# First turns of an attention pipeline: zeroing, first root and one weight split moved, unread products put into TensorE's gaps

## The chip, the cores and the metric

The kernel runs on one core of one Trainium2 chip. The metric is the device time of one launch in microseconds; the median of three runs is compared. The profile shows one further execution, taken by the hardware profiler.

## The reference

One transformer layer over 64 sequences of 128 tokens with a width of 512, in f32.

```python
h = base_weight[x] + lora_A.T[x] @ lora_B.T            # gather, rank 16
n = layernorm(h)                                       # no gain
cq, ckv = layernorm(n @ W_dq), layernorm(n @ W_dkv)   # 128 wide, with gain and bias
q, (k, v) = cq @ W_uq, ckv @ W_ukv                     # 16 heads of 32
h = h + softmax(causal(q k^T / sqrt(32))) v @ W_o.T
h = h + experts(layernorm(h))                          # shared expert and 8 of 16 routed experts
```

## The kernel before

The work falls into an attention phase (to about 943 us) and an expert phase. Both go over 16 groups of 4 sequences; a group is 512 tokens, four tiles of 128 rows. This document is about the first turns of the attention phase.

**Turns.** The attention phase is a software pipeline written out by hand: turn `n` runs from -2 to 16. A turn has 16 steps. In turn `n` the softmax of group `n` is done (16 slots, one a step: four heads of one tile), the `c` vectors of group `n + 1` are finished and its `q`, `k`, `v` begun, and the front of group `n + 2` is made: embedding `h`, its normalisation, the transposes `xt`, and the down projection `wd`. So turn -2 has only a front, for group 0; turn -1 has the front of group 1 and the first `ct`, `k` 0 and `q` 0 of group 0; turn 0 is the first one with softmax, and the output projection `out` begins in turn 1.

**Order of the work.** Each engine has its own instruction list with semaphores between them and works in order. Two banks of PSUM (`work`) pass the products of all parts of the front: `MIDWAY` and `END` say in which step a part comes, `place` gives the bank and how often it must have been drained, `empty` waits for that, and `was_read` frees it. TensorE's order of parts in turn -1 is `art` 0 and 1, `h` 0 to 3, `ct` 0 and 1, `k` 0, `xt` 0 to 2, `wd` 0, `xt` 3, `wd` 1, `q` 0. In turn 0 the `h` parts stand in steps 2, 3 and 5 between scores and transposes of probabilities.

**f32 products.** A product of f32 operands is made of three products of split operands (`split_matmul`, L487 to L489): each operand is stored as a rounded high part and the rest (`_hi`, `_lo`). The weights are split once at the start, in three pieces (`W_PIECES`): ScalarE rounds (L753) and VectorE subtracts (`split_weights`, L763). Pieces 0 and 1 arrive in the tile `k_diag`, piece 2 (the output projection's weights) in `res`.

**k_diag.** The keys are stored in a block-diagonal tile that must be zero where no key stands. GpSimd zeroes it once (L470), in step 8 of turn -2, behind the first gather for the next group; the first copies of `k` wait for it in turn -1.

**Root.** The inverse standard deviation is a seed from the exponent (`rsqrt_seed`, L66 to L71, four operations on VectorE) and three Newton steps of four dependent operations each (`rsqrt_steps`, L78 to L84), run by GpSimd in step 7 for `h` and in step 3 for `c`. The normalisation of `h` (L808, four operations, one a tile) waits for the whole of it.

**Gathers.** GpSimd issues four indirect DMAs a group (L439); the low-rank columns of the gathered rows are copied and split in `split_ar` (L769 to L772).

**Softmax in turn 0.** VectorE takes the row maxima for two slots at once (`row_max`, L877), ScalarE the exponentials (L698), VectorE the reciprocals (L883), GpSimd the scaling (L454), TensorE the transposes (L591), ScalarE the copies (L705), TensorE the products with `v` (L603).

Of the kernel before, what the change touches and what calls it, by code (L numbers as in the profile page):

```python
# [86 lines left out]
def shift_of(pool, done, count, mean, y, t, shift, passed):  # L87
# [28 lines left out]
END = {0: (("k", 1), ("q", 2)), 2: (("h", 0), ("h", 1)), 3: (("h", 2),), 4: (("v", 2),), 5: (("h", 3),)}  # L116
FRONT = ("art", "h", "xt", "wd")

STATS_AT, NORM_AT, C_NORM_AT, SPLIT_AT = (3, 6), 10, 5, 14
# [18 lines left out]
def is_turn(n, which):  # L138

    return isinstance(n, int) and n == which  # L140
# [78 lines left out]
def attention(nc, shared, w_ffn, w_gate, biases, table, tok, lora_b, w_attn, ln, h2):  # L219
# [3 lines left out]
    with ExitStack() as ctx:  # L223
# [127 lines left out]
        def was_read(instruction, n, part, i, drains=DRAINS):  # L351
            instruction.then_inc(work_free[place(n, part, i)[0]], drains)

        def slots_of(n):

            return range(0 if any(is_turn(n, k) for k in (-2, -1, GROUPS)) else SLOTS)
# [64 lines left out]
        @block.gpsimd  # L421
        def _(pool):
            pool.memset(ident[:, :], 0.0).then_inc(consts, 1)
            pool.memset(mask[:, :, :], 0.0).then_inc(consts, 1)
            pool.wait_ge(consts, 2)
            pool.affine_select(out=ident[:, :], in_=ident[:, :], compare_op=ALU.not_equal, fill=1.0,
                               base=0, pattern=[[-1, P]], channel_multiplier=1).then_inc(ident_done, 1)

            pool.affine_select(out=mask[:, :, :], in_=mask[:, :, :], compare_op=ALU.is_ge, fill=MASKED,
                               base=0, pattern=[[0, HPC], [-1, P]],  # L430
                               channel_multiplier=1).then_inc(ident_done, 1)
            pool.wait_ge(tok_step, 4)

            def pick(g):
                pool.tensor_copy(tok_now[:, :], tok_fix[:, bass.ds(g * TILES, TILES)]).then_inc(tok_picked, 1)
                wait_alone(pool, tok_picked, g + 1, pool_passed)

            def gather(g, t):
                pool.indirect_dma_start(  # L439
                    out=gath[:, t, :], out_offset=None, in_=table,  # L440
                    in_offset=bass.IndirectOffsetOnAxis(ap=tok_now[:, t:t + 1], axis=0),
                ).then_inc(gathered[t], 16)

            def wait_gathered(g):
                for t in range(TILES):
                    pool.wait_ge(gathered[t], 16 * (g + 1))

            def newton_of(base, n):
                rsqrt_steps(pool, newton, base, nw[:, 1, 0:n], nw[:, 3, 0:n], nw[:, 4, 0:n],
                            pool_passed)  # L450

            def normalise_probs(n, s):
                pool.wait_ge(inv_done, SLOTS * n + s + 1)
                pool.tensor_tensor(probs[:, s % RING, :, :], probs[:, s % RING, :, :],  # L454
                                   inv[:, s % RING, :].rearrange("p (h o) -> p h o", o=1).to_broadcast([P, HPC, P]),
                                   ALU.mult).then_inc(probs_done, 1)

            def turn(n, side):
                for step in range(SLOTS):
                    if has_slot(n, step - NORM_LAG):  # L460
                        normalise_probs(n, step - NORM_LAG)
                    if GATHER_AT <= step < GATHER_AT + TILES and has_part(n, "h", 0) and not is_turn(n, GROUPS - 3):
                        if step == GATHER_AT:
                            wait_gathered(n + 2)
                            drained(pool, n, "h", TILES - 1)
                            pick(n + 3)
                        gather(n + 3, step - GATHER_AT)
                        if is_turn(n, -2) and step == GATHER_AT:
                            pool.wait_ge(w_lo_done, len(W_PIECES))
                            pool.memset(k_diag[:, :, :, :, :], 0.0).then_inc(k_zeroed, 1)  # L470
                    if step == RSTD_AT and has_part(n, "xt", 0):
                        newton_of(2 * NEWTON_OPS * (n + 2), TILES)
                    if step == C_RSTD_AT and has_part(n, "ct", 0):
                        newton_of(2 * NEWTON_OPS * (n + 1) + NEWTON_OPS, 2 * TILES)

            pick(0)
            for t in range(TILES):
                gather(0, t)
            for n in range(-2, GROUPS + 1):
                turn(n, n % 2)  # L480

        @block.tensor
        def _(pe):
# [58 lines left out]
            def up(n, part, i):  # L542

                if is_turn(n, -1):
                    pe.wait_ge(w_lo_done, 2)
                elif is_turn(n, 0) and part == "v":
                    pe.wait_ge(w_lo_done, len(W_PIECES))
                if i == 0 and part != "v":
                    pe.wait_ge(cT_lo_done, 2 * (n + 1) + (1 if part == "q" else 2))
                if part == "v":  # L550
                    a, b = pair(cT_hi, cT_lo, 1, i * P, (i + 1) * P), wts(W_UV, D)
                else:
                    a = wts((W_UQ if part == "q" else W_UK) + i * P, P)
                    b = pair(cT_hi, cT_lo, int(part == "k"), 0, TOK)
                return split_matmul(bank_of(n, part, i), a, b, True, True)

            def out_proj(n, side, t, chunks=range(DC)):
                if not is_turn(n, GROUPS):
                    pe.wait_ge(oT_lo_done, DC * n)
                for m in chunks:  # L560
                    if is_turn(n, GROUPS):
                        pe.wait_ge(oT_lo_done, DC * (n - 1) + m + 1)
                    mm = split_matmul(bank_of(n, "out", t),
                                      pair(oT_hi[:, 1 - side], oT_lo[:, 1 - side], m, t * P, (t + 1) * P),
                                      wts(W_O + m * D, D), m == 0, m == DC - 1)
                return mm
# [27 lines left out]
            def heads_out(n, s):  # L594
# [10 lines left out]
                                   start=True, stop=True)  # L605
                mm.then_inc(o_full, 1)

            def work_on(n, side, uses):
                for part, i in uses:
                    if has_part(n, part, i):  # L610
                        empty(pe, n, part, i)
                        if part == "art":
                            mm = ar_turn(n, i)
                        elif part == "h":
                            mm = embed(n, i)
                        elif part == "xt":
                            mm = x_turn(n, i)
                        elif part == "wd":
                            mm = down(n, i)
                        elif part == "ct":  # L620
                            mm = c_turn(n, i)
                        elif part == "out" and is_turn(n, GROUPS) and i < 2:
                            mm = out_proj(n, side, i, range(2, DC))
                        elif part == "out":
                            mm = out_proj(n, side, i)
                        else:
                            mm = up(n, part, i)
                        mm.then_inc(work_full[place(n, part, i)[0]], 1)
# [130 lines left out]
        def _(dve):  # L759
# [33 lines left out]
            def seed_of(base, var, n):  # L793
                rsqrt_seed(dve, newton, base, var, nw[:, 0, 0:n], nw[:, 1, 0:n],
                           nw[:, 2, 0:n].bitcast(I32), nw[:, 4, 0:n])

            def h_seed(g):
                dve.wait_ge(h_moments, TILES * (g + 1))
                seed_of(2 * NEWTON_OPS * g, moments[:, :, 1], TILES)

            def c_seed(g):
                dve.wait_ge(c_moments, 2 * TILES * (g + 1))
# [122 lines left out]
            def turn(n, side):  # L925
                front, rows = has_part(n, "xt", 0), has_part(n, "ct", 0)
                for step in range(SLOTS):
# [24 lines left out]
                    if front:  # L952
                        if step == SPLIT_AT and is_turn(n, GROUPS - 2):
                            prepare_gate()
                        elif step == SPLIT_AT and not is_turn(n, GROUPS - 3):
                            split_ar(n + 3)
                        if step == STATS_AT[0]:
                            h_stat(n, 0)
                            h_stat(n, 1)
                        if step == STATS_AT[1]:  # L960
                            h_stat(n, 2)
                            h_stat(n, 3)
                            h_moment(n + 2)
                            h_seed(n + 2)
                            if is_turn(n, -2):
                                split_weights(2)
                        if step == NORM_AT:
                            normalise(n + 2)

            dve.memset(ar[:, :, :].bitcast(F32), 0.0).then_inc(ar_zeroed, 1)  # L970
            dve.wait_ge(tok_loaded, 16)
# [802 lines left out]
```

## Time and profile before

| | us |
|---|---|
| median of three runs | 2520.44 (2519.99 to 2520.92) |
| the profiled execution | 2518.29 |
| its span, first to last instruction | 2516.5 |
| TensorE busy | 2421.6 (96%) |
| ScalarE busy | 1814.8 (72%) |
| VectorE busy | 1707.6 (68%) |
| GpSimd busy | 1134.3 (45%) |
| mean granted TensorE clock | 0.995 |

PE is TensorE, PEld its weight loads, DVE VectorE, ACT ScalarE, POOL GpSimd and SP SyncE. Busy time is summed over instructions that the profiler recorded; matmuls are pipelined, so a product's duration includes its way through the array, and the distance between two starts says more. A time in the views below is counted from the span's start.

### The profile page before, as it was taken

Reading aid. Unit: us, or ns where it says so; the run is one execution under the profiler, and the core shown is the slowest. Engines: PE = TensorE matmul, PEld = TensorE weight load, DVE = VectorE, ACT = ScalarE, POOL = GpSimd, SP = SyncE. Lnnn points to the kernel's source line nnn. Section 1 sums busy time; section 2 is a strip of 40 time slices with the busy share of each in tenths; the row PEclk is TensorE's granted clock in tenths of the full one; section 3 lists DMA queues with packets and bytes.
Section 4 is the critical chain, followed back from the end, with each engine's and each line's share of the span. In section 5 each row is a group of like instructions: output and inputs, shape, how many; then the busy total and the mean of one; then the engine's idle time right before and its main releaser. Section 6 shows DMA issues by size and latency. Waiting matters only on the chain.

```text
span 2516.5 us, 47561 instructions
## 1 busy us (share of the span) xinstructions
PE 2421.6 (96%) x13632; PEld 1866.1 (74%) x13632; DVE 1707.6 (68%) x3604; ACT 1814.8 (72%) x4593; POOL 1134.3 (45%) x1285
## 2 busy tenths in 40 slices
PE   3899999999999999999999999999999999999999
PEld 2666666666666766678878878878878888888887
DVE  6777777777777764857657657657657657657655
ACT  1777777777777786868668668668668768767766
POOL 4444444444444332336436435445435445445445
PEclk8999999999999999999999999999999999999999
DMA  3222222222222122522222322221221321321321
GB/s 108 69 68 69 69 81 69 73 69 73 73 81 77 60 65 80 164 85 76 92 72 70 96 80 58 96 87 51 97 88 50 101 85 49 101 88 46 101 74 60
DMA packets 99830, 198.24 MB, mean 79 GB/s; under 512 B 10928, under 2 KB 10928, under 8 KB 99568
## 3 DMA queue, kind: packets, MB, share of 16 engines
q1 hardware_dynamic: 94576, 179.29, 21.6%
q0 software_dynamic: 5120, 17.31, 2.8%
q8 instruction: 67, 1.10, 0.2%
q14 instruction: 67, 0.55, 0.1%
HBM read 145.66 MB, written 50.86 MB: 78 GB/s over the span
## 4 chain that ended last, share of the span: by engine, by line
issue 30%; POOL 26%; PE 2%; DVE 1%; ACT 1%; POOLq 1%; DVEq 0%; ACTq 0%
POOL t_lo L1280 24%; POOL sh_lo L1280 2%; POOLq L1278 1%; DVE ps_u L1647 0%; DVE f_lo L1672 0%; DVE t L1654 0%; ACT t_hi L1499 0%; PE fwork L1295 0%; PE ps_g L1295 0%; ACT square L1482 0%; PE ps_g L1297 0%; PE ps_g L1296 0%; PE ps_u L1297 0%; PE ps_u L1295 0%; PE ps_u L1296 0%
## 5 line engine op out<-in xcount | busy, mean ns | idle before, releaser
L1280 POOL TENSOR_TENSOR t_lo<-t,t_hi 128x512 fp32r<-128x512 f32 x512 | 662.9, 1295 | 413.9 <-ACT t_hi L1499 413.8
L454 POOL TENSOR_TENSOR probs<-probs,inv 128x512 f32<-128x512 f32 x256 | 266.4, 1042 | 473.9 <-DVE inv L883 472.7
L1647 DVE TENSOR_TENSOR ps_u<-ps_u,square 128x512 f32<-128x512 f32 x512 | 357.0, 697 | 155.9 <-ACT square L1486 139.6
L1499 ACT ACTIVATE t_hi<-t 128x512 fp32r<-128x512 f32 x512 | 320.6, 626 | 112.0 <-PE ps_y L1297 66.8
L1654 DVE TENSOR_TENSOR t<-ps_u,res 128x512 f32<-128x512 f32 x512 | 354.0, 691 | 55.5 <-DVE ps_u L1647 22.4
L1482 ACT ACTIVATE square<-ps_g 128x512 f32<-128x512 f32 x544 | 319.6, 587 | 91.9 <-PE ps_g L1297 90.2
L698 ACT ACTIVATE probs<-ps_s,nmax 128x128 f32<-128x128 f32 x1024 | 364.0, 382 | 20.8 <-DVE nmax L877 19.7
L1486 ACT ACTIVATE square<-square 128x512 f32<-128x512 f32 x544 | 344.2, 633 | 17.3
L698 ACT ACTIVATION_READ_ACCUMULATOR probs<-ps_s,nmax 128x1 f32 x1024 | 228.0, 223 | 0.0
L1295 PE MATMUL ps_y<-t_hi,f_hi 128*128 128x512 f32 x512 | 208.4, 407 | 14.1 <-POOL t_lo L1280 12.6
L1280 POOL TENSOR_TENSOR sh_lo<-t,sh_hi 128x512 fp32r<-128x512 f32 x32 | 41.9, 1310 | 389.7 <-ACT sh_hi L1499 389.7
L1297 PE MATMUL ps_u<-xl_hi,f_lo 128*128 128x512 f32 x512 | 200.1, 391 | 0.0
L1296 PE MATMUL ps_y<-t_lo,f_hi 128*128 128x512 f32 x512 | 200.1, 391 | 0.0
L1295 PE MATMUL ps_u<-xl_hi,f_hi 128*128 128x512 f32 x512 | 199.9, 390 | 0.2 <-DVE t L1654 0.2
L1297 PE MATMUL ps_y<-t_hi,f_lo 128*128 128x512 f32 x512 | 199.9, 390 | 0.0
L1295 PE MATMUL ps_g<-xl_hi,f_hi 128*128 128x512 f32 x512 | 199.8, 390 | 0.0
L1297 PE MATMUL ps_g<-xl_hi,f_lo 128*128 128x512 f32 x512 | 199.5, 390 | 0.0
L1296 PE MATMUL ps_g<-xl_lo,f_hi 128*128 128x512 f32 x512 | 199.2, 389 | 0.0
L1296 PE MATMUL ps_u<-xl_lo,f_hi 128*128 128x512 f32 x512 | 199.2, 389 | 0.0
L705 ACT ACTIVATE pT<-ps_t 128x512 f32<-128x512 f32 x256 | 158.4, 619 | 27.3 <-PE ps_t L591 25.2
L877 DVE TENSOR_REDUCE nmax<-ps_s 128x8 f32<-128x1024 f32 x128 | 155.9, 1218 | 27.4 <-PE ps_s L582 26.9
L591 PE MATMUL ps_t<-ident,probs 128*128 128x128 f32 x1024 | 163.9, 283 | 8.1 <-ACT pT L705 4.9
(196 smaller groups left out, 5367.7 us busy)
## 6 DMA issues: line engine op xcount, KB each, us to landing
res<-w_rows SPq DMA_DIRECT2D x256, 256.0 KB, 3.2
h<-rows SPq DMA_DIRECT2D x64, 256.0 KB, 2.0
res<-h SPq DMA_DIRECT2D x64, 256.0 KB, 2.8
h<-res SPq DMA_DIRECT2D x64, 256.0 KB, 2.0
rows<-h SPq DMA_DIRECT2D x16, 1024.0 KB, 5.6
keep<-h SPq DMA_DIRECT2D x16, 1024.0 KB, 7.2
out<-keep SPq DMA_DIRECT2D x64, 256.0 KB, 2.3
keep<-in_w_ffn SPq DMA_DIRECT2D x12, 512.0 KB, 3.6
```

What stands on the lines that cost most here:

```text
L454: pool.tensor_tensor(probs[:, s % RING, :, :], probs[:, s % RING, :, :], inv[:, s % RING, :].rearrange("p (h o) -> p h o", o=1).to_broadca ...
L591: mm = pe.transpose(ps_t[:, j * P:(j + 1) * P], probs[:, s % RING, j, :], ident[:, :])
L698: e = act.activation(probs[:, s % RING, j, :], ps_s[:, b, x, i, y, :], ACT.Exp, bias=nmax[:, b, x, i, y:y + 1], accum_out=total[:, s % RIN ...
L1280: pool.tensor_tensor(lo, t[:, t_slot(j), :], hi.bitcast(F32), ALU.subtract).then_inc(t_lo_done, 1)
L1295: pe.matmul(o, a_hi, b_hi, start=first, stop=False)
L1296: pe.matmul(o, a_hi, b_lo, start=False, stop=False)
L1297: return pe.matmul(o, a_lo, b_hi, start=False, stop=last)
L1482: act.activation(square[:, j % 2, :], ps_g[:, j % 2, :], ACT.Relu).then_inc(relu_done, 1)
L1486: act.activation(square[:, j % 2, :], square[:, j % 2, :], ACT.Square).then_inc(square_done, 1)
L1499: act.activation(dst, t[:, t_slot(j), :], ACT.Copy).then_inc(t_hi_done, 1)
L1647: dve.tensor_tensor(dst, product, square[:, j % 2, :], ALU.mult).then_inc(t1_done, 1)
L1654: dve.tensor_tensor(t[:, t_slot(j), :], ps_u[:, u_bank(j), :], w_all[:, e % 2, :], ALU.mult).then_inc(t_done, 1)
```

## The change

- The zeroing of `k_diag` moves from step 8 of turn -2 to the start of GpSimd's list, behind the four gathers of group 0. It waits for two weight splits there instead of three.
- The Newton steps of the first `h` root (turn -2) are done by VectorE, right behind its seed, instead of by GpSimd. All later roots stay on GpSimd.
- VectorE's split of weight piece 2 moves from step 6 of turn -2 to step 1 of turn 0. The wait of TensorE for this piece moves from the `v` products of turn 0 to the first output projection in turn 1.
- `keep_awake` puts products on TensorE whose result nothing reads: in turn -1 ten before `ct` 0, eight before `k` 0 and four before `xt` 0, into the bank `ps_t`; in turn 0 two before each of the four `h` parts, into `ps_o`. Each multiplies the bf16 identity with the 128x512 bf16 mask.

```diff
+AWAKE = {("ct", 0): 10, ("k", 0): 8, ("xt", 0): 4}
...
+        def before_softmax(n):
+
+            return is_turn(n, -2)
...
                         gather(n + 3, step - GATHER_AT)
-                        if is_turn(n, -2) and step == GATHER_AT:
-                            pool.wait_ge(w_lo_done, len(W_PIECES))
-                            pool.memset(k_diag[:, :, :, :, :], 0.0).then_inc(k_zeroed, 1)
-                    if step == RSTD_AT and has_part(n, "xt", 0):
+                    if step == RSTD_AT and has_part(n, "xt", 0) and not before_softmax(n):
                         newton_of(2 * NEWTON_OPS * (n + 2), TILES)
...
                 gather(0, t)
+            pool.wait_ge(w_lo_done, 2)
+            pool.memset(k_diag[:, :, :, :, :], 0.0).then_inc(k_zeroed, 1)
...
                     pe.wait_ge(w_lo_done, 2)
-                elif is_turn(n, 0) and part == "v":
-                    pe.wait_ge(w_lo_done, len(W_PIECES))
...
             def out_proj(n, side, t, chunks=range(DC)):
+                if is_turn(n, 1) and t == 0:
+                    pe.wait_ge(w_lo_done, len(W_PIECES))
...
+            def keep_awake(bank, count):
+
+                for k in range(count):
+                    pe.matmul(bank, ident_b[:, :], mask[:, :, :], start=True, stop=True)
+
             def work_on(n, side, uses):
                 for part, i in uses:
                     if has_part(n, part, i):
+                        if is_turn(n, -1) and (part, i) in AWAKE:
+                            keep_awake(ps_t[:, :], AWAKE[part, i])
+                        if is_turn(n, 0) and part == "h":
+                            keep_awake(ps_o[:, :], 2)
                         empty(pe, n, part, i)
...
+            def newton_of(base, n):
+                rsqrt_steps(dve, newton, base, nw[:, 1, 0:n], nw[:, 3, 0:n], nw[:, 4, 0:n], dve_passed)
+
             def h_seed(g):
                 dve.wait_ge(h_moments, TILES * (g + 1))
                 seed_of(2 * NEWTON_OPS * g, moments[:, :, 1], TILES)
+                if before_softmax(g - 2):
+                    newton_of(2 * NEWTON_OPS * g, TILES)
...
                             h_seed(n + 2)
-                            if is_turn(n, -2):
-                                split_weights(2)
                         if step == NORM_AT:
                             normalise(n + 2)
+                        if is_turn(n, 0) and step == 1:
+                            split_weights(2)
```

## Rows read from the trace of the kernel before

**Rows 1.** Windows: engine busy us (instructions), then granted clock, DMA share, GB/s.
```profile
30.00:50.00 20.00, 12.27 (x71) 10.64 (x71) 13.09 (x34) 3.85 (x7) 8.30 (x10) 0.99 0.22 54
50.00:70.00 20.00, 10.69 (x40) 8.29 (x40) 14.05 (x35) 5.11 (x8) 9.93 (x25) 0.50 0.32 95
...
77.29:128.31 51.02, 44.34 (x350) 30.07 (x350) 40.46 (x100) 41.94 (x160) 24.90 (x44) 1.00 0.21 64
128.31:182.00 53.69, 52.55 (x397) 36.65 (x397) 40.75 (x91) 42.67 (x163) 23.93 (x43) 1.00 0.25 80
```

**Rows 2.** Timeline of GpSimd, turn -2: start us, us, engine, line, operation, tiles.
```profile
10.26 2.51 POOL L439 DMA_INDIRECT gath<-in_table,tok_now  x1 [0.30 <-issue]
24.18 2.17 POOL L78 TENSOR_TENSOR nw<-nw 128x4 f32<-128x4 f32 x1 [11.42 <-DVE nw L71]
...
29.65 0.20 POOL L84 TENSOR_TENSOR nw<-nw 128x4 f32<-128x4 f32 x1
...
31.89 3.52 POOL L470 MEMSET k_diag<- 128x4096 f32 x1
```

**Rows 3.** Timeline of VectorE, turn -2; the last row from a narrower window.
```profile
15.74 0.20 DVE L769 CAST ar<-gath 128x64 fp32r<-128x64 f32 x1 [3.79 <-DMA gath<-in_table,tok_now]
...
23.93 0.17 DVE L71 TENSOR_SCALAR nw<-nw 128x4 int32<-128x4 int32 x1
24.01 2.28 DVE L763 TENSOR_TENSOR w_lo<-res,w_hi 128x2048 fp32r<-128x2048 f32 x1
29.89 5.81 DVE L808 TENSOR_SCALAR keep<-rows,moments,nw 128x512 f32<-128x512 f32 x4 [3.60 <-POOL nw L84]
...
31.27 4.43 DVE L808 TENSOR_SCALAR keep<-rows,moments,nw 128x512 f32<-128x512 f32 x1
```

**Rows 4.** Timeline of TensorE, turn -2.
```profile
36.35 1.12 PE L518 MATMUL work<-ident,keep 128*128 128x128 f32 x4 [3.82 <-DVE xT_lo L813]
```

**Rows 5.** Timeline of TensorE, turn -1.
```profile
54.82 1.94 PE L538 MATMUL work<-ident,c 128*128 128x128 f32 x8 [3.81 <-DVE c L831]
60.31 0.77 PE L487 MATMUL work<-cT_hi,w_hi 128*128 128x512 f32 x1 [3.55 <-DVE cT_lo L845]
...
65.83 1.11 PE L518 MATMUL work<-ident,keep 128*128 128x128 f32 x4 [0.63 <-DVE xT_lo L813]
...
70.23 0.28 PE L488 MATMUL work<-w_lo,xT_hi 128*128 128x256 f32 x1
...
71.18 0.60 PE L518 MATMUL work<-ident,keep 128*128 128x128 f32 x4
```

**Rows 6.** Timeline of VectorE in the expert phase, around two Newton steps.
```profile
1056.77 1.13 DVE L82 TENSOR_SCALAR fnw<-fnw 128x4 f32<-128x4 f32 x1
...
1059.35 0.15 DVE L78 TENSOR_TENSOR fnw<-fnw 128x4 f32<-128x4 f32 x1
...
1060.05 0.16 DVE L84 TENSOR_TENSOR fnw<-fnw 128x4 f32<-128x4 f32 x1
```

**Rows 7.** Timeline of VectorE, turn -1.
```profile
57.31 1.52 DVE L840 TENSOR_SCALAR cT<-work,gains 128x512 f32<-128x512 f32 x2
...
62.58 1.90 DVE L808 TENSOR_SCALAR keep<-rows,moments,nw 128x512 f32<-128x512 f32 x4
```

**Rows 8.** Timeline of GpSimd, turn -1.
```profile
61.59 0.20 POOL L84 TENSOR_TENSOR nw<-nw 128x4 f32<-128x4 f32 x1
...
62.78 2.17 POOL L439 DMA_INDIRECT gath<-in_table,tok_now  x1 [0.83 <-POOL tok_now L435]
```

**Rows 9.** Timelines of turn 0: TensorE twice, VectorE, ScalarE.
```profile
77.29 0.60 PE L577 MATMUL ps_s<-mask,ident_b 128*128 128x512 bf16 x2
...
86.72 0.60 PE L577 MATMUL ps_s<-mask,ident_b 128*128 128x512 bf16 x2
...
83.02 1.19 DVE L877 TENSOR_REDUCE nmax<-ps_s 128x8 f32<-128x1024 f32 x1
...
84.34 0.39 ACT L698 ACTIVATE probs<-ps_s,nmax 128x128 f32<-128x128 f32 x1
```

## The prediction

> **What bounds the kernel now.** I first cut the span into stretches by turn [rows 1]. In turn 1 (128.31 to 182 us) TensorE is busy 52.55 of 53.69 us, while before the softmax starts no engine is near full: TensorE does 12.27 us of the 20 from 30 to 50 and 10.69 of the 20 behind them, and VectorE, the busiest, has gaps too. Until turn 0 the kernel is a chain of single steps, and what this chain gains or loses moves all of the rest. Next I read each engine in order of time. In turn -2 the chain is gather, split of the low-rank columns, `h`, statistics, root, normalise, transpose, split, `wd`. The root is twelve dependent operations on GpSimd: its first took 2.17 us beside VectorE's third weight split, and the last ends at 29.85 [rows 2, 3]. Then VectorE normalises; the fourth tile begins at 31.27 and lasts 4.43 us, until just after GpSimd's zeroing of `k_diag` (31.89 to 35.41) has ended [rows 2, 3]. VectorE works in order, so the split of `xT` stands behind it, and TensorE's third transpose, which waits for that split, comes only at 36.35 [rows 4]. In turn -1 the granted clock is 0.50 (1.2 GHz) over the whole stretch from 50 to 70, after a stretch in which TensorE was idle two fifths of the time; it is 1.00 (2.4 GHz) in turns 0 and 1 [rows 1]. The `wd` products of turn -1 show the price: the first sixteen begin 0.21 us apart, the last eight, from 70.23 to 71.18, 0.119 [rows 5].
>
> **First root on VectorE, and the weight split out of the way.** Removed: GpSimd's 5.7 us (24.18 to 29.85). Added: the same twelve operations on VectorE. The expert phase runs a step of four there from 1059.35 to 1060.05, plus 0.16, so about 0.89 us a step [rows 6] and 2.7 for three. The seed's last operation starts at 23.93 [rows 3], so the root ends near 26.8 instead of 29.85: 3.1 us. The four gathers for turn -1 now go out beside it. One scalar operation of such a root took 1.13 us instead of 0.17 beside GpSimd's work [rows 6]; three of them held like that would cost 2.9. But the four normalises at 62.58, beside a gather issued at 62.78, took 1.90 us, and it was the gather that was stretched to 2.17 [rows 7, 8]. That is the nearer row, and I take nothing.
>
> **Zeroing at the start.** It waits for the second weight split and is queued behind the last gather's issue (10.26 + 2.51 = 12.77), so it runs from 12.8 to 16.3 [rows 2]. It no longer stands beside the normalise: from the start of normalise to the third transpose turn -1 needs 65.83 - 62.58 = 3.25 us [rows 5, 7], turn -2 needed 36.35 - 29.89 = 6.46 [rows 3, 4]. That gains 3.2 us. But the small casts of the gathered rows start at 15.74 [rows 3], inside the zeroing's new place. If it holds them as it held the fourth normalise, they start at 16.35, a loss of 0.6; if not, 0. The held normalise is the nearest row, so I take 0.6.
>
> The Trainium skill, SBUF — State Buffer, section "SBUF: two separate sides", speaks against both moves: GpSimd and VectorE lock one shared port pair for a whole instruction, whoever comes first, and VectorE needs it in a two-port mode. By this rule the casts are held, and so can be the root's three scalar operations behind the gathers; that is rival (e) below.
>
> Turn -2 comes to 3.1 + 3.2 - 0.6 = 5.7 us. Where in `wd` the clock rises is open; a slow product costs 0.094 more than a fast one, and with some eleven of 24 slow before, all fast would gain 1.0 and five more slow lose 0.5. I take 5.6 for turn -2, bounds 4.0 and 7.0.
>
> **Unread products in turn -1.** Ten before `ct` 0, eight before `k` 0, four before `xt` 0, each 128x512 in bf16. Two of that shape, the mask products, take 0.53 us at 2.4 GHz, the time to the next product [rows 9]; at the low level a product of 512 columns costs twice the 0.21 of one of 256. So ten cost 2.7 to 4.3 us, and TensorE is idle 3.81 before `ct` 0; eight cost 2.1 to 3.4 in a gap of 3.55; four cost 1.1 to 1.7 in one of 1.3 [rows 5]. Fast, all lie inside the gaps; slow, the first overruns by 0.5 and the last by 0.4. The ten and the `ct` products (1.94) make one dense stretch of 6 us, longer than the 4.4 between the third transpose at 65.83 and the first fast product at 70.23 [rows 5], so I expect the high level from `k` 0 on. What that buys: at `ct` nothing, since VectorE reaches the gains only at 57.31 [rows 7], after `ct` has ended at 56.76 [rows 5]. `k` 0 ends 0.7 earlier, and more would not help: the normalise at 62.58 next waits for GpSimd's second root, which ends at 61.79 [rows 7, 8]. From there to the end of `wd` 0 it was 71.18 - 62.58 = 8.6 us. The first transposes save 0.45 of it, the third one 0.4, and 24 fast products take 2.9 us instead of 4.5: 2.5 together. So 3.2 us for turn -1; bounds -0.5 (the clock stays low, the overrun is paid) and 4.0.
>
> **What turn 0 pays.** The third weight split (2.28 us) [rows 3] now stands on VectorE in front of the second row maximum at 83.02 [rows 9]. Behind that maximum stand the second reciprocal and two additions to `h`, and ScalarE's third exponentials wait for it. They go from 84.34 to 86.5. An `h` product needs the bank that the first addition frees, so it comes 1.4 us later, and the scores behind it start at 88.1 instead of 86.72 [rows 9]. GpSimd's first scaling and the transposes that wait for it lie inside the same delay. ScalarE is busy 41.94 of the turn's 51.02 us, VectorE 40.46 [rows 1], and in the first part of the turn in particular they hand work to one another without a pause, so I let nothing be made up. GpSimd's `c` root sits behind its third scaling and comes 2.0 late. The unread products, two before each `h`, cost 0.53 a pair: three pairs fall into waits, the last is added. For split and products together I take 2.0 us; below, 0.5 if the idle time on TensorE (51.02 - 44.34 = 6.7 us over the turn) takes it up; above, 2.3 + 4 x 0.53 = 4.4.
>
> The waits that the change adds for the third split cost nothing: the first load of `res` queues on SyncE behind the stores of `h` of the same turn, which are later than the split's new end near 85.3, and the output projection comes in turn 1. What used to cover the split was the wait for GpSimd's root; that cover is gone, and its whole price is in turn 0's term.
>
> **Sum.** -5.6 - 3.2 + 2.0 = -6.8 us. The profiled execution took 2518.29 us, 1.8 more than its span of 2516.5, so its successor would take 2511.5. The median of the runs is 2520.44, 2.15 above the profiled one; the forecast for the median is 2520.44 - 6.8 = 2513.6.
>
> **The rivals.** (a) The clock stays low in turn -1. For it: the unread products alone must lift it, and before them it had just fallen; against it: the dense stretch of 6 us. Then -5.6 + 0.5 + 2.0 = -3.1, 2517.3. (b) Turn 0's delay is paid at its upper bound, since VectorE, ScalarE and GpSimd hand the probabilities round in a fixed order; against it, the idle time on TensorE. Then -5.6 - 3.2 + 4.4 = -4.4, 2516.0. (c) The split's delay returns: if the fixed order throws 2.28 us in at four of the eight row maxima of turn 0, it costs 9.1, and the time is 2520.44 - 8.8 + 9.1 = 2520.7. Slower begins at 8.8 us lost in turn 0, slower by over 0.2% at 13.8; that TensorE is idle 6.7 us there and only one instruction is added speaks against it. (d) Everything falls well: the zeroing holds nothing, the clock is high early in both turns, turn 0 takes up the split: -7.0 - 4.0 + 0.5 = -10.5, 2509.9. (e) GpSimd's gathers hold the first root's scalar operations for 2.9 us, as the 1.13 us row would have it: -3.9, 2516.5; the normalise beside a gather speaks against it. That the change does nothing at all at the first root is all but excluded: VectorE's wait of 3.60 us before the normalise ends with GpSimd's last root operation [rows 3].
>
> **How the numbers follow.** The forecast has 0.55, (a) 0.15, (b) 0.12, (c) 0.03, (d) 0.10, (e) 0.05. A difference of 0.2%, 5.0 us, is about what a measurement of this kernel can tell from no change, so the border is at 2515.4. The forecast's own range is 2511.6 to 2515.6, nearly all of it faster, and (d) is faster too; (a), (b) and (e) lie within 0.2% with some of their spread beyond it. That gives faster 0.68, same 0.29, slower 0.03. The range of eight in ten goes up to half a microsecond beyond (a) and down to 2510.8, which leaves out (c) and most of (d): 2510.8 to 2517.8.
>
> **What would show it.** The casts at 16.35; normalise of turn -2 at about 27.4 and its four operations in 1.9 us; the third transpose near 30.7; the granted clock at 1.00 from `k` 0 of turn -1 on; the scores of turn 0 at about 68.5 instead of 77.29; turn 0 some 53 us long, and turn 1 as it was. The forecast is wrong if the root on VectorE takes over 4 us, if the low clock comes back behind the unread products, or if turn 0 grows by over 4 us or not at all.

## The result and the profile after

The median went from 2519.89 us (20 runs, 2517.65 to 2521.46) to 2516.1 us (20 runs, 2513.25 to 2519.15): 3.8 us less, ratio 0.9986, 95% interval 0.9980 to 0.9993. That is a small gain, clear of zero but within 0.2%. The forecast was 2513.6, range 2510.8 to 2517.8. The profiled execution took 2515.29 us with a span of 2513.5.

The runs of the change differ in TensorE's clock, and the time goes with it: the three with a mean granted clock of 0.999 took 2513.3 to 2514.6 us, the two with 0.998 took 2513.3 and 2516.9, the thirteen with 0.997, the profiled one among them, 2515.3 to 2518.0, and the two with 0.996 took 2518.5 and 2519.2. Times near the forecast came only at 0.998 and 0.999.

The main reading is the lead of the changed kernel at landmarks, its start time against that of before. Turn -2 first; this is the timeline of VectorE in the changed kernel, its line numbers shifted a little against before:

```profile
15.46 0.20 DVE L782 CAST ar<-gath 128x64 fp32r<-128x64 f32 x1 [3.47 <-DMA gath<-in_table,tok_now]
...
23.83 0.17 DVE L71 TENSOR_SCALAR nw<-nw 128x4 int32<-128x4 int32 x1
24.03 0.16 DVE L78 TENSOR_TENSOR nw<-nw 128x4 f32<-128x4 f32 x1
...
26.57 0.16 DVE L84 TENSOR_TENSOR nw<-nw 128x4 f32<-128x4 f32 x1
26.77 1.95 DVE L826 TENSOR_SCALAR keep<-rows,moments,nw 128x512 f32<-128x512 f32 x4
```

The root takes 2.7 us (24.03 to 26.73) and nothing holds it, though a gather was issued at 24.12 and one at 25.37: the two scalar operations beside them take 0.17 us each. In the seed before it one scalar operation did take 0.34 instead of 0.17 us and ended with the issue of the gather of 22.85. The normalise starts 3.12 us earlier and takes 1.95 instead of 5.81 us [rows 3]. The timeline of GpSimd has the zeroing, which ends at 15.57, as the casts begin:

```profile
12.06 3.51 POOL L482 MEMSET k_diag<- 128x4096 f32 x1 [0.90 <-DVE w_lo L776]
```

TensorE's third transpose, at 30.04, is 6.31 us ahead of [rows 4]. Turn -1 on TensorE:

```profile
44.83 3.16 PE L615 MATMUL ps_t<-mask,ident_b 128*128 128x512 bf16 x9 [0.33 <-issue]
48.33 1.16 PE L542 MATMUL work<-ident,c 128*128 128x128 f32 x8 [0.35 <-DVE c L849]
49.33 1.89 PE L615 MATMUL ps_t<-mask,ident_b 128*128 128x512 bf16 x8
53.82 0.77 PE L491 MATMUL work<-cT_hi,w_hi 128*128 128x512 f32 x1 [2.60 <-DVE cT_lo L863]
...
55.24 1.93 PE L615 MATMUL ps_t<-mask,ident_b 128*128 128x512 bf16 x4
56.97 1.15 PE L522 MATMUL work<-ident,keep 128*128 128x128 f32 x8
59.17 0.66 PE L522 MATMUL work<-ident,keep 128*128 128x128 f32 x4 [1.05 <-DVE xT_lo L831]
...
62.74 0.60 PE L522 MATMUL work<-ident,keep 128*128 128x128 f32 x4
```

The ten products (nine are recorded) run from 44.8, and the clock is up from 46.9, but the eight end at 51.2, TensorE idles 2.60 us, and at 53.8 the clock falls again, so `k` 0 runs at the low level: it gains nothing over [rows 5]. Behind it the clock is up from 57.2, and the whole of `wd` 0 is fast: from the normalise at 56.09 to the transpose at 62.74 it takes 6.65 us instead of 8.6. The scores of turn 0 begin at 69.14, 8.15 us ahead of [rows 9] (8.4 in truth: the first of the two mask products is not recorded here, at both ends of the turn, so the turn's length is right). The windows, columns as in [rows 1], the last one being turn 0 from its first scores to those of turn 1:

```profile
30.00:50.00 20.00, 16.19 (x85) 11.66 (x87) 12.59 (x45) 3.47 (x7) 2.54 (x12) 0.91 0.12 46
50.00:70.00 20.00, 15.36 (x91) 10.97 (x92) 11.88 (x41) 6.88 (x12) 8.25 (x17) 0.91 0.27 62
69.14:124.92 55.78, 47.34 (x353) 31.42 (x356) 42.81 (x98) 42.38 (x162) 26.87 (x44) 0.97 0.19 58
```

Turn 0 is 55.78 us long instead of 51.02, so 4.8 of the 8.15 us are given back there. The lead is 3.4 us at the start of turn 1 (128.31 against 124.92), 3.0 at the end of this span, 3.8 between the medians. Where it goes at first is seen on VectorE and GpSimd:

```profile
74.64 2.26 DVE L776 TENSOR_TENSOR w_lo<-res,w_hi 128x2048 fp32r<-128x2048 f32 x1
76.82 1.22 DVE L895 TENSOR_REDUCE nmax<-ps_s 128x8 f32<-128x1024 f32 x1
```

```profile
74.81 2.99 POOL L459 TENSOR_TENSOR probs<-probs,inv 128x512 f32<-128x512 f32 x1 [12.59 <-DVE inv L901]
```

The line of the same scaling before:

```profile
83.18 1.04 POOL L454 TENSOR_TENSOR probs<-probs,inv 128x512 f32<-128x512 f32 x1 [14.48 <-DVE inv L883]
```

The split holds the row maximum behind it (76.82 against 83.02, so 6.2 us of the lead are left) and GpSimd's first scaling, which takes 2.99 instead of 1.04 us. The lead falls to 5.71 at the third scores (81.01 against 86.72, [rows 9]). A second loss stands later in the turn, in the two splits of `c` on VectorE:

```profile
100.61 2.77 DVE L863 TENSOR_TENSOR cT_lo<-cT,cT_hi 128x512 fp32r<-128x512 f32 x2
```

```profile
105.70 1.29 DVE L845 TENSOR_TENSOR cT_lo<-cT,cT_hi 128x512 fp32r<-128x512 f32 x2
```

The second line is from before, where the same two took 1.29 us. And the clock is low from 98.1 to 101.6, which in turn 0 of before it never was.

### The profile page after: what moved, and what is told of

It reads as the page before. It is cut to its first block, busy times and chain, and to the rows that moved or that the text cites. A ratio compares the mean times of both kernels' runs of the same rounds, so it can differ in the third digit from the quotient of the medians.

```text
span 2513.5 us, 47538 instructions
## 1 busy us (share of the span) xinstructions
PE 2419.0 (96%) x13583; PEld 1866.6 (74%) x13662; DVE 1707.5 (68%) x3616; ACT 1815.3 (72%) x4593; POOL 1130.6 (45%) x1273
## 4 chain that ended last, share of the span: by engine, by line
issue 30%; POOL 26%; PE 2%; DVE 1%; ACT 1%; POOLq 1%; DVEq 0%; ACTq 0%
POOL t_lo L1298 24%; POOL sh_lo L1298 2%; POOLq L1296 1%; DVE ps_u L1665 0%; DVE f_lo L1690 0%; DVE t L1672 0%; ACT t_hi L1517 0%; PE fwork L1313 0%; PE ps_g L1313 0%; ACT square L1500 0%; PE ps_g L1315 0%; PE ps_g L1314 0%; PE ps_u L1315 0%; PE ps_u L1313 0%; PE ps_u L1314 0%
```

## Experiments

Twelve kernels, in three groups of four, each group timed beside the kernel before on a chip of its own; the change was timed apart from them. "Turn 0" is the distance from its first scores to those of turn 1 in the one profiled execution. The runs of one kernel scatter over 3 to 8 us, so differences of less than 1.5 us between two medians are not resolved; the lengths of turn 0 are sharper, but one execution each, and the clock differs from execution to execution. "Gap" is the third weight split in VectorE's gap of turn -2.

| kernel | median against before, us | ratio, 95% interval | scores of turn 0 at | turn 0, us |
|---|---|---|---|---|
| before | | | 77.29 | 51.02 |
| the change | -3.8 | 0.9986 (0.9980 to 0.9993) | 69.14 | 55.78 |
| split in a gap | -5.1 | 0.9978 (0.9969 to 0.9987) | 70.91 | 53.87 |
| no products in turn 0 | -1.1 | 0.9995 (0.9986 to 1.0004) | 69.82 | 57.96 |
| no products | +0.8 | 1.0002 (0.9993 to 1.0011) | 71.82 | 57.83 |
| gap, no products | -5.0 | 0.9978 (0.9968 to 0.9987) | 72.41 | 51.05 |
| products of turn -1 alone | -3.0 | 0.9991 (0.9982 to 1.0000) | 76.13 | 51.09 |
| gap, products of turn -1 | -7.8 | 0.9972 (0.9962 to 0.9982) | 69.29 | 52.71 |
| gap, products of turn 0 | -3.6 | 0.9987 (0.9978 to 0.9996) | 71.08 | 53.85 |
| the change, five products in step 9 | -1.7 | 0.9992 (0.9983 to 1.0001) | 69.57 | 55.82 |
| gap, turn -1, later gathers | -7.9 | 0.9969 (0.9958 to 0.9980) | 71.39 | 51.27 |
| the same, 16 before `k` 0 | -8.0 | 0.9967 (0.9955 to 0.9979) | 69.30 | 51.21 |
| the change, later gathers | -4.7 | 0.9982 (0.9973 to 0.9991) | 70.13 | 57.05 |
| gap, no products, zeroing back | -1.7 | 0.9993 (0.9984 to 1.0002) | 76.09 | 51.07 |

**Split in a gap.** The third weight split moves out of turn 0 to step 13 of turn -2.

```diff
-                        if is_turn(n, 0) and step == 1:
+                        if is_turn(n, -2) and step == 13:
                             split_weights(2)
```

> The change, with the third weight split in step 13 of turn -2 instead of turn 0; VectorE idles 3.2 us there (32.6 to 35.8) waiting for ScalarE's copy of c. Theory T (turn 0 loses 4.8 us mostly because the split stands in front of its second row maximum): the scores of turn 0 start at 69.1 as in the changed kernel, turn 0's normalise comes 2.5 to 3.5 us earlier than 105.7, and the time is 6 to 7 us below before. Rival R (the unread products of turn 0 cost it) and rival S (an early start is absorbed in turn 0 whatever stands there): 3.8 below before, as the changed kernel.

Its turn 0 is 53.87 us, 1.9 shorter than the change's. The split itself runs inside VectorE's wait for ScalarE's copy of `c`, and 2.08 us of the wait are still there behind it. So beside the products the split costs turn 0 1.9 us, and turn -2 nothing. Theory T fell: the normalise of turn 0 came at 105.56, not 2.5 to 3.5 us before 105.7, and the median gained 1.3 over the change, not 2.2 to 3.2; in this profile the lead at turn 0 was 1.8 smaller, since the clock was low from 56.2 to 63.0 in turn -1. The split is a part of the loss and not most of it.

```profile
32.47 2.28 DVE L776 TENSOR_TENSOR w_lo<-res,w_hi 128x2048 fp32r<-128x2048 f32 x1
36.83 0.29 DVE L839 BATCH_NORM_STATS2 cstats<-c 128x6 f32<-128x128 f32 x1 [2.08 <-ACT c L687]
```

**No unread products in turn 0, and none at all.** The first drops the two lines with `ps_o`, the second also those with `ps_t`.

> The change without the eight unread products of turn 0. T: only the pair before the last h counts, 4.3 below before. R: the four pairs cost 2 to 4 us, so 6 to 8 below before. S: 3.8 below.

> The change without any unread products. T: turn -1 loses the 1.7 to 2.0 us that the high clock gave there and turn 0 gains 0.5: 2.3 below before. R: 4 to 6 below before. S: turn 0 absorbs what turn -1 loses, 3.8 below before. The scores of turn 0 should start near 71 instead of 69.1 in all of them.

All of the expectations fell: both are slower than the change. Turn 0 is 2.2 and 2.1 us longer than the change's. Behind the split's wait the clock falls, as the windows of TensorE show for the kernel without the eight (busy, then granted clock):

```profile
76.00:78.00 2.00, 0.72 (x2) 1.00 0.02 4
78.00:80.00 2.00, 0.81 (x5) 0.75 0.00 0
80.00:82.00 2.00, 2.00 (x4) 0.50 0.62 230
82.00:84.00 2.00, 2.00 (x7) 0.50 0.09 34
84.00:86.00 2.00, 2.00 (x11) 0.54 0.34 129
```

So the eight products of turn 0 are needed because of the split. What the split costs without them is seen against the kernels with it in the gap: 5.3 us of turn 0 where turn -1 has its products (57.96 against 52.71), 6.8 us where there are none at all (57.83 against 51.05, the next kernel). The second pair was timed side by side, and its medians are 5.8 us apart: this is the best resolved effect of all.

**Gap and no products: the root and the zeroing alone.** The split in the gap, and no `ps_t` or `ps_o` lines.

> Root on VectorE and zeroing at the start alone: no unread products, the third split in VectorE's gap at step 13 of turn -2. T: the lead of 6.3 us that the changed kernel has at the third transpose of turn -2 goes through to the end, 6 below before. S: about 3.8 or less below before, since turn 0 absorbs part of any early start.

Turn 0 is 51.05 us, the length of before, and the lead of 4.9 us that it starts with is there at the start of turn 1 (4.85) and in the median, -5.0; at the end of this one span it is 4.1. This refutes the theory that turn 0 absorbs an early start. The lead was 4.9 and not 6.3: normalise starts at 27.10 instead of 26.77, with the casts held for 0.4 us (15.42 to 16.0), so the third transpose is 5.98 ahead; the rest went in the rows of 24 `wd` 0 products, in which the clock rose later than before, in turn -2 behind some 17 of them instead of 11, in turn -1 behind 20 instead of 16.

**Products of turn -1 alone,** `AWAKE` and its two lines put into the kernel before.

> The kernel before with the 22 unread products of turn -1 and nothing else. Theory T (what turn -1 gains is kept as long as TensorE's wait for the copy of the probabilities in step 9 of turn 0 stays at 2.0 us and the clock stays up): scores of turn 0 start 1.9 us earlier than 77.3, turn 0 is 51.0 us long, the time is about 1.9 below before. Rival S (turn 0 absorbs an early start): no difference from before.

Turn 0 begins 1.2 us earlier and keeps its length. The median says -3.0 with an interval that reaches to 0, so it fits both 1.2 and the expected 1.9.

**Gap, with the products of one turn.** The split in the gap, and only the `ps_t` lines, or only the `ps_o` lines.

> The change with the third split in VectorE's gap of turn -2 and with no unread products in turn 0; those of turn -1 stay. T: scores of turn 0 start at 69 to 71, turn 0 is 51.0 us long (nothing delays it, and the clock stays at its high level around 98 us), 6.5 to 8 us below before. Rival S: as with no unread products at all, 5.0 below before.

> Third split in the gap of turn -2, no unread products in turn -1, the eight of turn 0 kept. T: the eight products cost 0.9 us directly and lengthen TensorE's wait in step 9 from 1.97 to 2.3 us, behind which the clock falls for some 4 us; turn 0 is 53.9 us long instead of 51.0 and the time is about 2 below before. Rival U (the fall of the clock in turn 0 belongs to the earlier start, not to the eight products): turn 0 is 51.9 long and the time 4 below before.

With those of turn -1 the median is 7.8 us below before, twice the gain of the change; turn 0 is 52.71 long, and the clock fell in it all the same (95.3 to 98.7). With those of turn 0 it is 53.85 long. So where no split stands in the turn, the eight products only cost: 1.2 us (53.87 against 52.71, both with those of turn -1; the medians, -5.1 and -7.8, point the same way). In the median the kernel with the products of turn 0 is 3.6 below before, near rival U's 4 and not T's 2, though its turn 0 has the length that T gave. T was wrong in one point more: the fall of the clock near 98 us does not need the eight. What decides about it is not shown: TensorE's wait ahead of it is 2.01 us in the kernel with the products of turn -1, but 1.98 in the kernel with later gathers below, where the clock falls too, and 1.97 to 1.99 in five kernels where it stays up (before; gap, no products; products of turn -1 alone; 16 before `k` 0; zeroing back).

**Five more products in step 9,** ahead of TensorE's wait before that fall.

```diff
+                    if is_turn(n, 0) and step == 9:
+                        empty(pe, n, "ct", 0)
+                        keep_awake(bank_of(n, "ct", 0), 5)
                     if TURN_FIRST and has_slot(n, step - T_LAG):
```

> The change plus five unread products in step 9 of turn 0, ahead of the wait for the copy of the probabilities, into the empty bank of the ct part. T: the clock stays at its high level from 98 to 102 us, and 1.5 to 2 us come back: 5.5 below before. If the low stretch costs nothing (ScalarE and VectorE set the pace there anyway): 3.8 below, as the changed kernel.

The clock now stays at 1.00, and turn 0 is as long as before the edit, 55.82 us. The time that the products gain is waited away in front of the `k` product, which stands 2.81 us for VectorE's splits of `c`. So in this execution the low clock there is not what costs. The median of -1.7 bears out neither expectation; the profiled run is not typical, 1.8 us below the median with a mean clock of 0.998, while seven of the eleven runs have 0.996 or 0.997. The two with 0.999 took 2512.8 and 2513.4 us, the two with 0.996 took 2519.7 and 2520.0. The windows of the change and of this kernel:

```profile
98.00:100.00 2.00, 2.00 (x10) 0.54 0.03 8
100.00:102.00 2.00, 2.00 (x11) 0.61 0.13 19
```

```profile
98.00:100.00 2.00, 2.00 (x17) 1.00 0.00 0
100.00:102.00 2.00, 1.40 (x12) 1.00 0.00 0
```

**Later gathers.** The durations of the two splits of `c` in turn 0 and the start of GpSimd's first gather beside them gave the next theory. In the kernel before the splits begin at 105.70 and take 1.29 us, while the gather issued at 105.98 is stretched to 1.34; in the change the gather begins first (100.09), takes 1.06, the next scaling of probabilities follows it at once, and the splits (100.61) take 2.77 us. The same order goes with the same durations in all ten kernels to here: 1.29 us in the three where the splits are first, 1.98 to 2.96 in the seven where the gather is. The edit moves the gathers of turn 0 by one step.

```diff
-                    if GATHER_AT <= step < GATHER_AT + TILES and has_part(n, "h", 0) and not is_turn(n, GROUPS - 3):
-                        if step == GATHER_AT:
+                    gather_at = GATHER_AT + is_turn(n, 0)
+                    if gather_at <= step < gather_at + TILES and has_part(n, "h", 0) and not is_turn(n, GROUPS - 3):
+                        if step == gather_at:
```

> Third split in VectorE's gap of turn -2, unread products in turn -1 only, and GpSimd's four gathers of turn 0 one step later (steps 9 to 12). Theory P (the rest of turn 0's loss is the order of GpSimd's first gather and VectorE's two splits of c: in the three kernels where the split comes first it takes 1.29 us for two, in the seven where the gather is first 1.98 to 2.96): the split takes 1.29 us again, turn 0 is about 51.2 long instead of 52.7, 8.5 to 9 us below before. Rival C (the low clock behind step 9 is the cause): turn 0 keeps its length if the clock still falls there, 7.7 below before.

The second kernel adds eight more products, 16 in all, ahead of `k` 0 of turn -1; the third has the later gathers on the change as it stands.

> The kernel before this one in the list, with 16 unread products instead of 8 ahead of k 0 of turn -1. Theory: TensorE waited another 2.6 us idle there and the clock fell at 53.8; now it stays high through k 0, which ends 0.6 to 0.9 earlier, and 0.3 more comes from the four behind it: about 1 us below the kernel with 8. Rival: if they run at the low level they end 2.5 us after k 0 could have begun, and it is 1 to 2 us above.

> The change as it is, with the gathers of turn 0 one step later. P: VectorE's splits of c take 1.29 instead of 2.77 us, turn 0 is 54.3 long instead of 55.8, 5.3 below before. C: 3.8 below before, as the change.

In the first, turn 0 is 51.27 us instead of 52.71, although the clock is low again from 97.6 to 101.1, for as long as without the edit. Of these 1.4 us, 1.16 are the splits' own; some 0.3 were there when they began, since the clock fell inside the `ct` products in the one kernel (they took 1.53 us) and behind them in the other (1.09). The median did not follow: -7.9 against -7.8, where P expected -8.5 to -9 and C -7.7. So the price of the order rests on the profiled turns alone. VectorE and GpSimd, the kernel with the split in the gap and the products of turn -1, without and with later gathers:

```profile
98.06 2.63 DVE L861 TENSOR_TENSOR cT_lo<-cT,cT_hi 128x512 fp32r<-128x512 f32 x2
```

```profile
98.00 1.06 POOL L444 DMA_INDIRECT gath<-in_table,tok_now  x1 [0.82 <-POOL tok_now L440]
99.08 1.05 POOL L459 TENSOR_TENSOR probs<-probs,inv 128x512 f32<-128x512 f32 x1
```

```profile
99.62 1.47 DVE L862 TENSOR_TENSOR cT_lo<-cT,cT_hi 128x512 fp32r<-128x512 f32 x2
```

```profile
101.36 1.06 POOL L444 DMA_INDIRECT gath<-in_table,tok_now  x1 [0.82 <-POOL tok_now L440]
```

This is the rule of the Trainium skill, SBUF — State Buffer, section "SBUF: two separate sides", in its other clause: VectorE with two inputs in SBUF and GpSimd reading SBUF exclude each other, and who is first has the ports for the whole instruction. The rows agree for the scaling: the first of the two splits (98.06, beside the gather's issue) takes 0.69 us, the second begins at 98.66 and ends at 100.69, 0.56 us behind the scaling's end at 100.13. So what holds the splits here is the scaling, which follows the gather at once; the gather's place decides when it comes. In the second kernel, with 16 products before `k` 0, the wait there is 0.88 us instead of 2.36, the clock is up from `ct` to the end of turn 0, and the scores of turn 0 begin at 69.30; its median, -8.0, is 0.1 below the kernel with eight and not the 1 us that was expected, and can't be told from the two beside it. In the change as it stands (the third) the splits take 1.36 us, as expected, but in the profiled execution the clock fell in the split's wait at 79.6 in spite of the eight products, and turn 0 took 57.05 us; the median of -4.7 lies between the expectations. So the eight products hold the clock in some executions and not in others, and the later gathers are neither borne out nor refuted by this kernel.

**Zeroing back** in step 8 of turn -2, on the kernel with root and gap alone.

> Root on VectorE, third split in the gap, no unread products, and the zeroing back in step 8 of turn -2 behind the first gather (waiting for two weight splits). The kernel with the zeroing at the start was 5.0 below before. If the zeroing holds VectorE's scalar operations while it runs (23.8 to 27.3), the root ends at about 29 instead of 26.7 and the lead at the third transpose of turn -2 shrinks from 6.3 to about 4: 2.7 below before. If only the large normalise was held by it, nothing stands there any more and it is 5.0 below before.

It gives back 3.7 us at the scores of turn 0 (76.09 against 72.41) and 3.3 in the median, more than the 2.3 that were expected if the zeroing holds scalar operations. It holds even the small ones of the seed, here the first two (128x4) for 4.1 us, the first 0.5 of them beside the issue of the gather ahead of it:

```profile
23.18 4.12 DVE L66 TENSOR_SCALAR nw<-moments 128x4 f32<-128x4 f32 x1
23.26 4.05 DVE L67 TENSOR_SCALAR nw<-moments 128x4 f32<-128x4 f32 x1
23.74 3.53 POOL L475 MEMSET k_diag<- 128x4096 f32 x1
27.34 0.17 DVE L69 TENSOR_SCALAR nw<-nw 128x4 int32<-128x4 int32 x1
```

## Why the prediction held, and where its sum was off

The time lies in the stated range, but two of the three signs of being wrong that the prediction set itself came true: the low clock came back behind the unread products, and turn 0 grew by over 4 us. The front of the chain came as described and 0.7 us better than forecast; the terms of turn -1 and turn 0 were off by 1.35 and 2.8 us the other way, which the range was wide enough to hold.

- **The start as a chain.** Right. A lead that reaches turn 0 goes through where turn 0 keeps its length (gap and no products: 4.9 us at its start, 4.85 at its end, 5.0 between the medians).
- **Root and zeroing, 5.7 us.** Root 3.1 forecast, 3.12 measured; to the third transpose 3.2 forecast, 3.19 measured. The loss of 0.6 at the casts did not come in the profile of the change, where the zeroing ended 0.1 us behind the first cast's start. It did come, at 0.4 us, in the kernel with gap and no products, where it ended at 15.95 and the first cast took 0.58. So the sign and the mechanism were right and the size depends on when the zeroing starts: 12.06, not 12.8, as the last gather's issue was not stretched to 2.51 this time and the zeroing waited only for the second weight split. Rival (e) fell by its size: none of the root's three scalar operations was held, and the one of the seed that was lost 0.2 us, not 2.9.
- **Turn -1, 3.2 us.** 1.85 measured (lead 6.3 to 8.15; 2.1 with the product that is not recorded). The step that failed is "high level from `k` 0 on": the ten products lifted the clock as said, but after the eight had ended TensorE was idle for 2.60 us and the level fell at 53.8, so the 0.7 at `k` 0 did not come. With 16 instead of eight the level held, in the one profile of that kernel. `wd` was fast all through, 1.95 of the expected 2.5.
- **Turn 0, 2.0 us.** This is the term that was mis-sized: it measured 4.8 us. The prediction made its 2.0 of 1.4 for the split, at the scores behind the first addition to `h`, and 0.53 for one pair of products. Measured by taking one thing away after another, the split costs 1.9 (55.78 to 53.87) and the eight products 1.2 (to 52.71), where three of the four pairs had been said to fall into waits. What the prediction did not have at all is GpSimd's scaling ahead of VectorE's splits of `c`: the order costs up to 1.4 (to 51.27). Together 4.5 of 4.8, each step from one execution.
- **The near hit of rival (b) is luck.** It gave 2516.0 for a measured 2516.1, from -5.6, -3.2 and +4.4. The profile has -6.3, -1.85 and +4.8. Its mechanism, an order of hand-overs that does not forgive, is right in kind, but its working (the split and all eight products in full) leaves the order of scaling and splits out and counts each product in full.
- **The chances.** Faster than 0.2% had 0.68; the result lies within 0.2%, which had 0.29.

What stays open: how much of the 4.8 us falls on each part in other executions, since the clock in turn 0 differs from run to run; what turned the order of the gather and the splits round, which no experiment isolates (beside the earlier start, the products of turn -1, those of turn 0 or the split in turn 0 each do it; the earlier start alone and the products of turn -1 alone do not); and what decides whether the clock falls near 98 us.

## What to carry to other kernels

Put a long elementwise operation where its engine waits for another, not merely off the old critical path: the same 2.3 us cost nothing at one place and 1.9 to 6.8 us of turn 0 at the other, by whether the clock fell behind them. Fillers for the clock paid here in turn -1, where TensorE's own speed set the end of `wd`, and against a long wait that the change itself had made; in turn 0 without that wait they only cost. The three kernels with the split in the gap, fillers in turn -1 and none in the softmax turn were the best, 7.8 to 8.0 us below before, twice the gain of the change, and can't be told apart. After any shift of the start, look for pairs of VectorE and GpSimd instructions whose order has turned round.

## What the runs showed of the hardware

- A half-microsecond shift of GpSimd against VectorE decides who waits: 1.29 us for VectorE's two splits of `c`, or up to 2.96 with GpSimd's scaling ahead of one of them.
- A 3.5 us zeroing on GpSimd delays a VectorE operation on four columns by 4 us. The issue of a gather did so by 0.2 us (0.34 instead of 0.17) for one operation and not at all for others beside it.
- A low clock need not cost: in two profiled executions turn 0 took 55.78 us with 3.4 us at the low level and 55.82 without, since the time went into a wait behind it. Over whole runs it did go with the time: 2513.3 to 2514.6 us at a mean clock of 0.999, 2518.5 and 2519.2 at 0.996.
